# A decoder layer: k projected one slot earlier, denominators summed and inverted one to two slots earlier, mixes behind the weighted product

## What is computed

```
x_prev = the x of the batch row before (zeros for the first)
k = (mu_k*x + (1-mu_k)*x_prev) @ Wk.T      (v and r in the same way)
exp_k = exp(k); exp_k_v = exp_k * v
denominator_out = Sd + exp_k * exp(u)       Sd' = Sd*decay + exp_k
numerator_out   = Sn + exp_k_v * exp(u)     Sn' = Sn*decay + exp_k_v
x1 = layernorm(x + (sigmoid(r) * numerator_out / denominator_out) @ W_out.T)
```

## Time and profile before

| | |
|---|---|
| median of three runs | 1133.65 us (1131.59 to 1134.21) |
| profiled execution | 1138.07 us, its span 1136.2 us |
| PE busy | 1003.7 us (88%) |
| DVE busy | 770.1 us (68%) |
| ACT busy | 687.3 us (60%) |
| POOL busy | 640.1 us (56%) |
| mean granted TensorE clock | 0.966 |

### The profile page before, as it was taken

How to read it: one execution, slowest core, us unless ns; L and a number is a source line. 1 busy time by engine, 2 the same in 40 slices (tenths; PEclk the granted TensorE clock), 3 DMA queues, 4 the chain that set the end, 5 groups by cost and what they waited for, 6 DMA issues and landing times.

```text
span 1136.2 us, 21749 instructions
## 1 busy us (share of the span) xinstructions
PE 1003.7 (88%) x6580; PEld 767.1 (68%) x6580; DVE 770.1 (68%) x1631; ACT 687.3 (60%) x2182; POOL 640.1 (56%) x683
## 2 busy tenths in 40 slices
PE   3779989989898988987989889888899999999995
PEld 2456666667666666765767666666778888887784
DVE  2378787797977978779797887976432222355586
ACT  1187766766667566665766667677345565566633
POOL 5565476466765567665476664322355555566654
PEclk9799999999999999998999999999999999999998
DMA  9622253333443331111311111021344555588766
GB/s 254 217 86 85 80 159 122 120 100 104 146 140 115 105 104 56 40 51 52 108 45 50 46 38 39 28 67 51 112 126 129 152 157 149 165 261 273 249 190 196
DMA packets 97871, 135.38 MB, mean 119 GB/s; under 512 B 11202, under 2 KB 83553, under 8 KB 97760
## 3 DMA queue, kind: packets, MB, share of 16 engines
q1 hardware_dynamic: 84704, 101.53, 29.8%
q0 software_dynamic: 13056, 32.47, 7.8%
HBM read 61.91 MB, written 76.23 MB: 122 GB/s over the span
## 4 chain that ended last, share of the span: by engine, by line
PE 50%; DVE 26%; issue 11%; ACT 6%; POOL 3%; DMA 2%; SPq 1%; another core or an unknown queue 0%; DVEq 0%; POOLq 0%; ACTq 0%
PE bM L564 8%; DVE Sc L1298 7%; PE four L817 6%; PE bT L817 6%; PE four L858 5%; PE four L743 4%; PE bT L578 4%; DVE wkv L1275 4%; PE bU L709 3%; PE bO L779 2%; ACT QT L1030 2%; DVE st L1213 2%; DVE nmx L1300 2%; ACT Sc L1038 2%; PE four L799 1%
## 5 line engine op out<-in xcount | busy, mean ns | idle before, releaser
L1038 ACT ACTIVATE Sc<-Sc,nmx 128x256 f32<-128x256 f32 x512 | 252.8, 500 | 29.2 <-DVE nmx L1300 29.2
L1046 ACT ACTIVATE PT<-bT 128x512 f32<-128x512 f32 x256 | 150.9, 589 | 153.2 <-PE bT L578 152.4
L1298 DVE TENSOR_SCALAR Sc<-four 128x1024 f32<-128x1024 f32 x128 | 156.1, 1219 | 106.2 <-PE four L743 92.3
L1694 POOL DMA_INDIRECT Yt<-PT,dests x150 | 149.3, 996 | 107.3 <-issue 57.9
L578 PE MATMUL bT<-idn,Sc 128*128 128x128 f32 x1024 | 167.1, 287 | 20.2 <-ACT PT L1046 17.6
L578 PEld LDWEIGHTS bT<-idn,Sc 128*128 128x128 f32 x1024 | 116.1, 144 | 94.9 <-issue 57.1
L1300 DVE TENSOR_REDUCE nmx<-Sc 128x4 f32<-128x1024 f32 x128 | 156.2, 1220 | 4.4
L1677 POOL DMA_INDIRECT Xs<-x,slots x120 | 119.9, 999 | 35.2 <-issue 18.3
L564 PE MATMUL bM<-mix,Wp 128*128 128x256 f32 x384 | 99.2, 403 | 30.5 <-POOL mix L1632 8.6
L1613 POOL TENSOR_TENSOR rstd<-vpe,mhalf 128x2 f32<-128x2 f32 x48 | 35.5, 739 | 127.4 <-DVE vpe L1221 127.4
L564 PEld LDWEIGHTS bM<-mix,Wp 128*128 128x128 f32 x384 | 72.5, 199 | 48.1 <-issue 28.4
(11 more groups left out here) (217 smaller groups left out, 2056.7 us busy)
## 6 DMA issues: line engine op xcount, KB each, us to landing
Xs<-yg SPq DMA_DIRECT2D x16, 1768.0 KB, 8.2
xb<-Xs SPq DMA_DIRECT2D x152, 136.0 KB
yg<-Yt SPq DMA_DIRECT2D x30, 512.0 KB
W<-w SPq DMA_DIRECT2D x4, 1152.0 KB, 11.5
xTs<-xT SPq DMA_DIRECT2D x16, 256.0 KB, 3.2
x<-x SPq DMA_DIRECT2D x16, 256.0 KB, 2.9
Base<-stg SPq DMA_DIRECT2D x15, 256.0 KB
yg<-Base SPq DMA_DIRECT2D x30, 128.0 KB
```

The costliest lines, as they stand in the source:

```text
L1038: last = fn(Sc[:, n % 3, m, t, :], Sc[:, n % 3, m, t, :], ACT.Exp, bias=nmx[:, n % 3, m, t:t + 1], accum_out=rs[:, s % 2, t, h:h + 1])
L1046: fn(flat(PT[:, h % RING]), bT[:, :], ACT.Copy).then_inc(a_pt.sem, 1)
L1298: ts(Sc[:, n % 3].rearrange("p m t k -> p (m t k)"), flat(score_banks(n)), CLAMP, -CLAMP, ALU.min, ALU.max).then_inc(d_clip.sem, 1)
L1694: pool.indirect_dma_start(Yt, bass.IndirectOffsetOnAxis(ap=dests[:, i % IDS, b:b + 1], axis=0), y_rows(i)[:, b, :], None, bounds_check=SPA ...
```

## The change

Five things are moved, and four waits are added for them:

1. PE and ACT: the product of k (`first_part(b, 0)`) and `exp_k(b)` go from slot 5 to slot 4. The product waits for the copy of the transposed x1 instead of the copy of q, since that is now the bank's last reader.
2. PE: `project_q(a)` goes behind the first transpose of slot 5 and also waits for `exp_k(b)`, which now uses the bank before it. The product of v waits for `copy_q`.
3. POOL: `sums` is split. The denominator's half (`sum_den`) goes in front of the third part of `send`; the numerator's half (`sum_num`) stays after slot 6. `state` goes in front of `add_bo`.
4. DVE: `invert` goes from the end of slot 7 to slot 5, behind the router's first part.
5. POOL: `mixes(b)` waits until `finish_wkv(a)` is done.

No instruction is added or removed. The diff:

```diff
@@ PE, first_part, n == 0
-                        pe.wait_ge(a_q.sem, a_q.at(s - 1))
+                        pe.wait_ge(a_x1T.sem, a_x1T.at(s - 1))
@@ PE, first_part, n == 1
                     pe.wait_ge(a_ek.sem, a_ek.at(s))
+                    if s:
+                        pe.wait_ge(a_q.sem, a_q.at(s - 1))
@@ PE
             def project_q(s):
                 pe.wait_ge(a_x1T.sem, a_x1T.at(s))
+                if s + 1 < L:
+                    pe.wait_ge(a_ek.sem, a_ek.at(s + 1))
@@ PE, slot
+                if heads:
+                    turn_probs(n, 0)
                 if A and g == 5:
                     project_q(a)
-                if heads:
-                    turn_probs(n, 0)
...
-                if B and g == 5:
+                if B and g == 4:
                     first_part(b, 0)
@@ ACT, slot
+                if B and g == 4:
+                    exp_k(b)
                 if T and g == 5:
                     t_chunk(t, 5)
-                if B and g == 5:
-                    exp_k(b)
@@ DVE, slot
                     router(t, 0)
+                if B and g == 5:
+                    invert(b)
...
-                if B and g == 7:
-                    invert(b)
@@ POOL, mixes
                     pool.wait_ge(p_kvr.sem, p_kvr.at(s - 1))
+                    pool.wait_ge(d_wkv.sem, d_wkv.at(s - 1))
@@ POOL
-            def sums(s):
+            def sum_den(s):
                 pool.wait_ge(a_ek.sem, a_ek.at(s))
-                pool.wait_ge(d_ekv.sem, d_ekv.at(s))
+                if s:
+                    pool.wait_ge(d_wkv.sem, d_wkv.at(s - 1))
                 by = eu[:, :].rearrange("p (j a) -> p j a", a=1).to_broadcast([P, ND, TOK])
                 pool.tensor_tensor(den, ek, by, ALU.mult).then_inc(g_den.sem, 1)
                 pool.wait_ge(g_den.sem, g_den.at(s, 1))
                 pool.tensor_tensor(den, den, Sd, ALU.add).then_inc(g_den.sem, 1)
+            def sum_num(s):
+                pool.wait_ge(d_ekv.sem, d_ekv.at(s))
+                if s:
+                    pool.wait_ge(p_wout.sem, p_wout.at(s - 1))
+                by = eu[:, :].rearrange("p (j a) -> p j a", a=1).to_broadcast([P, ND, TOK])
                 pool.tensor_tensor(num, ekv, by, ALU.mult).then_inc(g_den.sem, 1)
...
@@ POOL, step
+                if A and a + 1 < L:
+                    state(a)
                 if A:
                     add_bo(a)
                 pairs(4)
-                if A and a + 1 < L:
-                    state(a)
+                if B:
+                    sum_den(b)
                 send(s - 2, 2)
                 pairs(5)
                 send(s - 2, 3)
                 pairs(6)
                 if B:
-                    sums(b)
+                    sum_num(b)
```

## The result

| | before | changed |
|---|---|---|
| median of four runs | 1132.62 us (1129.89 to 1134.21) | 1097.53 us (1094.82 to 1097.89) |
| profiled execution, span | 1138.07 us, 1136.2 us | 1097.59 us, 1095.8 us |
| PE busy | 1003.7 us (88%) | 980.7 us (89%) |
| DVE busy | 770.1 us (68%) | 775.0 us (71%) |
| mean granted TensorE clock | 0.966 | 0.982 |

The changed kernel takes 0.9687 of the time before, 95% interval 0.9662 to 0.9713: 35.1 us less. 1088.3 us had been predicted, with a range of 1079 to 1109. The time is in the range, but 9.2 us above the forecast and outside the forecast's own range (1083 to 1094), so something in the sum is wrong. (The diff adds five waits, not the four that are announced ahead of it: for `copy_q`, for `exp_k`, twice for `finish_wkv`, in `mixes` and in `sum_den`, and for `project_out` in `sum_num`.)

What follows compares the result with a forecast made beforehand. DVE and PE were taken to set the pace in turn, with 3.2 us of reciprocals where DVE is late. Gains of 38.1 (ordinary steps) + 4.5 + 0.9 + 1.8 = 45.3 us gave a median of 1088.3 us, range 1079 to 1109.

Steps and rivals of the forecast that it cites:

- The bound and the first half of a step: From DVE's `finish_wkv` (formerly `invert`) after slot 7 to PE's `project_q` point: DVE sets the pace; 26.75 us become 22.75.
- The second half: From PE's old `project_q` point to DVE's next `finish_wkv`: 21.3 us become 21.55, a loss of 0.25.
- The clock: TensorE's half-level stretch around the scores disappears as PE's 1.44 us pause shrinks; 1.1 of 1.59 us a step arrive.
- What removes `finish_wkv`'s slowness: DVE after slot 7: with `invert` gone and no `mixes` beside it, `finish_wkv` takes 1.4 us; with reciprocals it was 6.0.
- The start: First row through step 1: earlier `finish_wkv` and less ACT waiting, less a small loss, together gain 1.8 us.
- Step 10: The step with the planner on DVE: its first instructions come 4.6 us sooner, a gain of 4.5 us.
- A: Rival: PE still pauses enough and the clock still falls once a step, 12 x 1.1 us missing: 1101 us; 17%.
- C: Rival: POOL's `sum_den` and DVE's router block one another for a whole 1.27 us instruction, 0.7 a step: 1097 us; 9%.
- B: Rival: ACT's 3.4 us hide nothing and the clock gives back all 1.59 us a step: 1082 us; 6%.
- D: Rival: in slot 5 ACT's queue waits for q before the exponentials, losing 2 us a step: 1116 us; 8%.
- E: Rival: `project_q` waits on `exp_k`, that on POOL's `state` behind `send`; slower than before, 1148 us at 6 us; 4%.

Runs made afterwards that it cites:

- before_again: The kernel before, unchanged, run once more for a trace on the same chip as other follow-ups: 1141.29 us (one run).
- e4: The changed kernel with `invert` alone put back at the end of slot 7: 1128.83 us, ratio 0.9894 to the kernel before.
- changed_again: The changed kernel, unchanged, run once more as the measure for others on its chip: 1109.16 us, ratio 0.969 to the kernel before.
- e5: The kernel before with one edit, `mixes` wait for `finish_wkv`: 1110.87 us, ratio 0.974 to the kernel before.
- e1: The changed kernel without the wait of `mixes` for `finish_wkv`: 1110.02 us, ratio 0.9697 to the kernel before.
- e6: The kernel before with only k's product and `exp_k` in slot 4, q behind the transpose, `state` ahead of `add_bo`: 1156.33 us, ratio 1.0112.
- e2: The changed kernel with `mixes` waiting for `finish_wkv` only from row 2 on: 1111.76 us, ratio 0.9711 to the kernel before.
- e3: The changed kernel with rows 0 and 1 in the old order, only `sum_den` split off; `mixes` wait from row 2 on: 1104.13 us, ratio 0.9652.
- e8: e3 with ACT's `copy_q` behind the first two exponentials in slot 5: 1087.56 us, ratio 0.960 to the kernel before.
- e7: e8 with DVE's `weigh_k` ahead of the router's second part in slot 6: 1094.46 us, ratio 0.9677 to the kernel before.

## Why the prediction was right or wrong

**The bound and the first half of a step: right.** DVE at T0 was what set the pace, and 22.32 us were measured for the 22.75 forecast, through the same steps: `project_out` last before `add_x`, then ACT's copy and exponentials, and 3.45 us to R.

**The second half: right.** 21.66 us for 21.55. q is read out from R + 4.6 (forecast 4.4), the reciprocals start at R + 5.1 (4.85), the clip at R + 8.4 (8.1), the transpose of slot 6 at R + 9.1 (8.95) after a PE pause of 1.30 us (1.2), the product of r at R + 15.2 (14.9).

**The clock: right in its outcome, mis-sized, and its reason not shown.** I took 2.9 us of the step's gain from DVE, less 0.25 in the second half, and 1.1 from the clock. The steps at either level give 1.8 us for the clock (before_again, 46.2 and 48.0; 1.57 in e4) and 2.2 for the pace (46.2 to 43.98, on different chips; 1.8 if changed_again's 44.35 is taken). The two errors nearly cancel. The reason, that the clock stays up because the 1.44 us pause shrinks, is contradicted in part: in e5 the pause is unchanged and the clock stays up in eight of eleven steps; in e4 it falls every second step. Nor is it the other pause, of 1.14 us before the scores 12.7 us behind the mark, which e4, e5 and the changed kernel lack: before_again's steps at full clock have it. What decides it stays open. Where a mean clock of 0.96 over 47 us meets 1.57 us of time lost in e4, the Trainium skill's estimate (TensorE: Matmul & The Clock Gate, Terms) would be 1.9 us. The 0.96 is rounded, and by windows of half a microsecond it is 0.964, which makes the estimate 1.7 us; the 1.57 of e4 and the 1.8 of before_again lie on either side of it.

**What removes `finish_wkv`'s slowness: only half understood.** I counted 1.4 us for it after the change, which was right, and gave `mixes`' wait and `invert`'s move as its joint cause. e1 and e5 show that either one is enough: each alone keeps `finish_wkv` and `mixes` apart. On top of the wait (0.974) all the rest of the change gives 0.005, some 5 us, though the intervals overlap, and the wait on top of the rest (0.9697) gives nothing that can be measured. In between, k's early product costs 13 us (e6 against before) to 18 us (e4 against e5, 0.9894 and 0.974; e4 has the split sums as well), and `invert`'s move gives 23 us back (e4 against changed).

**The start: the step that failed.** The profiled execution is 4.8 us above the 1092.8 forecast for it: +10.9 from the start, +2.2 from step 10, +0.1 from step 14, -3.6 from the eleven ordinary steps, -4.7 from the rest. Against the medians the rest's 4.7 falls away, as it is nearly all the excess of before's profiled execution over its median. So the start is the largest part: -1.8 us predicted, +9.1 in the profiled pair, about +5 in the other executions. The step read "Together 1.8": a gain of 1.3 from the first row, of 0.68 in step 0 and a loss of 0.25 in step 1. I applied the steady step's terms to steps in which their covers are missing:

- First row: I put `finish_wkv` 2.3 us early, counting the reciprocals and a late `weigh_k`, but not that `finish_wkv` also needs `tanh_r`, and that through the product of r waits for `weigh_k`. Counted from `exp_k` it is between 0.6 us late and 0.2 early. The 2.7 us are there only where `invert` stays behind `weigh_k` (e4: 8.4 us for 11.1).
- Between rows 0 and 1 `state` runs beside the norm (2.17 us for 0.73), and q waits for `exp_k` (0.78 us).
- In step 0 ACT is last, and the wait for q costs 1.7 us instead of gaining 0.7.
- In step 1 `state` has no sends ahead of it and meets the norm: 2.4 us instead of 0.25.

e6 shows that the early k with its `state` makes 7.6 us of loss by itself, e4 that the early `invert` takes away the first row's gain, and e2 that the wait of `mixes` isn't the cause. e3 undoes 4.5 us, all ahead of the second `add_x`, and leaves the last two columns as they are. For the columns three and four the place is named by rows and, for `copy_q`, by e8; that `state` beside the norm causes the fourth was not tried by itself.

**Step 10: half, in this pair of executions.** The planner's instructions do come earlier, but into the time of `mixes`, as the rows above show. I had looked at when PE waits for them, not at what would run beside them. This is read from rows, of e5 as well, where only `mixes` are later; it was not tried by itself.

**The rivals.** A (the clock still falls once a step, 1101) lies close to the time but is not what happened: steps 2 to 9 and 11 to 13 show 1.00. C was right as a mechanism: beside `sum_den` the router's two instructions take 1.01 and 1.21 us where they took 0.19, 1.8 us lost for the 1.27 I had priced, and the same in every ordinary step. (The prediction's 0.94 for the worst product of `finish_wkv` mixes the two: they lost 0.70 and 0.88 us.) That is the rule of the Trainium skill (SBUF — State Buffer, Who interferes with whom), and this trace agrees with it. The reciprocals start 0.25 us later than forecast, and no more, as they wait for `sum_den` anyway; so not 0.7 us. B was right as a mechanism, too: the clock is worth 1.6 to 1.8 us a step and not 1.1, and R comes 0.43 us sooner than forecast, but the start hides it in the total. D and E did not happen: e8 gets back 0.27 us a step from ACT's order in slot 5, so that order didn't cost 2, and `state` is done before `exp_k` wants it.

## What to carry to other kernels

Before moving work, look at whether the slow instruction merely has a neighbour it need not have: one wait that keeps POOL's `mixes` away from DVE's `finish_wkv` gave 29 of 35 us, while the elaborate part of the change had to earn back what it cost. Cost a moved step in the start and in the odd step by their own rows, since the covers of the steady step are absent there, and keep the old order where they are. When an instruction is to come earlier, go through all that it waits for: here the reciprocals came sooner, and a third input, `tanh_r`, came later for it. For every instruction that becomes earlier or later, ask what the other engine does at that time: four places here (`finish_wkv`, the router, the planner, the norm) gained or lost 0.6 to 2.7 us by that alone.

## What was not expected of the hardware

- A tiny instruction loses as much as a large one: 128x8 elements take 1.02 us for 0.17 (e7), 128x32 take 1.21 for 0.19, 128x16 take 1.07 for 0.23, each beside a POOL instruction of 1.0 to 1.3 us. Not every DVE instruction loses: the clips, which read PSUM, keep their 1.22 us beside `mixes`, and so do the maxima's reductions.
- The clock can fall in every second of otherwise equal steps (e4), or begin to fall in the middle of a run of equal steps (before_again, from step 6 on), with PE's longest pause the same 1.44 to 1.45 us.
- Equal steps at full clock come in several lengths. The changed kernel's profiled execution has 43.98 us throughout, changed_again 44.04 once, 44.8 twice and then 44.35. Of the last difference, 0.34 us lies between the starts of `context_v` and `project_out`, 3.92 and 4.26 us; why is open. It makes differences of 0.3 us a step between kernels uncertain where they ran on different chips.
- Two executions of the same kernel differ by 4.7 us at the mark of step 1 (147.07 and 142.40), and 3.4 us of this are four PE groups that met the half level (13.4 us for 9.9).
